# The second expert stage of a four-layer network made sparse: rows scattered to tiles of their experts, weights addressed by a register

## The chip, the cores and the metric

One core of a Trainium2 chip. The metric is the time of one execution on the device, in microseconds (us). Everything is fp32 except where bf16 is named.

## What is computed

Four layers over x (4 batches of 512 rows of 128) and a context (4 x 154 x 128). Each layer is a cross-attention (L2 adds causal self-attention) and a feed-forward part of experts, both added to x by a gate. The two expert stages that the change touches most:

```python
# L0: 8 experts, top 2, at most C = 1.25 S / E rows an expert; h = relu(x w1 + b1); out = h w2 + b2
# L1: 8 experts, top 2, no limit on an expert's rows
router_logits = x_flat @ gate_w                       # (2048, 8)
router_probs = softmax(router_logits)
top_k_probs, top_k_idx = top_k(router_probs, 2)       # then normalized to sum 1
gate_up = einsum('nd,edh->enh', x_flat, gate_up_w)    # gate_up_w (8, 128, 512)
hidden = silu(gate_up[..., :256]) * gate_up[..., 256:]
expert_out = einsum('enf,efd->end', hidden, down_w)   # down_w (8, 256, 128)
output = sum over the 2 chosen experts of expert_out * top_k_probs
# L3: 16 experts, top 2, and a shared expert
```
x_flat is the layer normalization of the residual rows. L2's and L3's experts stay dense in both kernels.

## The kernel before

The rows stand in SBUF all the time (`resid`, 16 tiles of 128 rows; a batch is QT = 4 tiles). `build` runs one block of instructions after another: setup, and for each layer an attention block (L0x, L1x, L2x with L2a, L3x) and an expert block (L0f, L1f, L2f, L3f); each ends with a barrier of all engines (L2991, L2993), so that no engine enters a block before all have left the one ahead of it. In a block each engine has its own list, written by hand, and semaphores tie them.

**L0f, sparse already.** `Dispatch` finds for each row the slots of its two experts: DVE takes the two best logits (`best`), TensorE counts the ranks with triangular matmuls (`ranks`), DVE turns them into slot numbers (`place`). `scatter` (L2091 to L2100) lets POOL write each tile of 128 rows twice with an indirect DMA into `slots_in` in DRAM, 32 in all, in three groups of tiles, `GROUPS` = (0, 8), (8, 12), (12, 16). The first group's 16 stand in the attention block L0x, whose POOL then waits until they have landed (L926). `sparse_experts` (L2121) loads the slots by SP, and its results go to `slots_out`; the next block, `wide_attention` of L1x (L232), gathers each row's two results by indirect DMAs on POOL and adds them (L593 to L749).

**L1f, dense.** `Router` (L1571) does the routing of one batch of 4 tiles at a time; the first batch's is hosted in L1x (`router.` hooks at L299, L409 and after). `experts` (L1706) goes through 32 items, a batch and an expert each: `up(item + 1)`, then `down(item)` on TensorE. An item is 2 units of 128 hidden columns; a unit is two 128x512 matmuls (L1774, L1775: weights stationary, 512 rows moving) into one of two pairs of PSUM banks, a silu on ACT (L1823) and a product on DVE (L1872). Down (L1788) is 8 matmuls, and DVE adds the expert's share with the routing weight (L1884, L1887). After a batch's last item `update_rows` (L732 to L749) adds the gated sum to the rows and takes the statistics for the next normalization (BATCH_NORM_STATS2, the centering of `resid`, BATCH_NORM_AGGREGATE).

**The end.** L3f is the same `experts` with 17 items a batch (its `rowsT` is L1646); after it `store` (L2780) writes all of `resid`, 1 MB, in a block of its own.

What `up` does in the dense stage:

```python
for k, (wg, wu, rows) in enumerate(items[item % NI][0]):
    n = units_to(item) + k
    if n >= SETS:
        pe.wait_ge(s["hid"], n - SETS + 1)
    nc.tensor.matmul(psum[0:rows, 2 * (n % 2), :], wg, xnT[b % 2][:], start=True, stop=True)
    nc.tensor.matmul(psum[0:rows, 2 * (n % 2) + 1, :], wu, xnT[b % 2][:], start=True, stop=True).then_inc(s["up"], 1)
```

## Time and profile before

| | |
|---|---|
| median of 3 runs | 1821.96 us (1820.03 to 1822.71) |
| profiled execution, its own time | 1822.82 us |
| its span, first to last instruction | 1821.1 us |
| TensorE (PE) busy | 1466.5 us, 81% of the span |
| VectorE (DVE) busy | 1058.4 us, 58% |
| ScalarE (ACT) busy | 683.6 us, 38% |
| GpSimd (POOL) busy | 394.6 us, 22% |
| mean busy share of the DMA engines | bytes moved 32.17 MB, mean 18 GB/s |
| granted TensorE clock, mean | 0.88 of full speed |

A share of busy time is a mean over all blocks, and each block has its own limit. A matmul of fp32 shows as more than one record. "Idle before" counts an engine's idle time just ahead of an instruction, and the name after it is what ended that. PEq and the like are an engine's own sequencer. SPq rows are DMAs that SP issued.

### The profile page before, as it was taken

How to read it: one execution, taken by the hardware profiler on the slowest of the kernel's cores; microseconds unless marked ns; L12 is line 12 of the kernel's file. 1: busy time of each engine (PE TensorE's matmuls, PEld its weight loads, DVE VectorE, ACT ScalarE, POOL GpSimd, SP SyncE). 2: the span in 40 equal slices, each digit the busy share in tenths (PEclk: the TensorE clock that was granted, in tenths of full speed). 3: DMA queues.
4: the chain of work that ended last, by engine and by line, in shares of the span. 5: the costliest groups of instructions: out<-in, count | busy, mean ns of one | idle time of the engine just before them, and what ended most of it. 6: DMA issues, size and time to landing. Idle time of an engine off the chain costs nothing. (4 is left out here: it accounts for less than half of the span.)

```text
span 1821.1 us, 26968 instructions
## 1 busy us (share of the span) xinstructions
PE 1466.5 (81%) x9930; PEld 886.7 (49%) x9930; DVE 1058.4 (58%) x2645; ACT 683.6 (38%) x1824; POOL 394.6 (22%) x488
## 2 busy tenths in 40 slices
PE   3677925758989979995888599888888968887997
PEld 2333414535556546664333356565554544344564
DVE  6555541154556656655454576676775964556886
ACT  3233412246656422223334355555552133332111
POOL 1000042345323300000100276767550001000000
PEclk7677867979999989996799699999998977988999
DMA  2430011140000000001000000000000010000000
GB/s 48 141 121 14 8 42 56 37 101 12 2 1 1 1 1 1 0 1 22 7 9 2 1 1 1 1 1 1 1 1 1 1 22 8 9 2 1 1 1 24
DMA packets 46823, 32.17 MB, mean 18 GB/s; under 512 B 16076, under 2 KB 41109, under 8 KB 46693
## 3 DMA queue, kind: packets, MB, share of 16 engines
q1 hardware_dynamic: 42885, 25.43, 5.6%
q0 software_dynamic: 2048, 4.20, 1.0%
q8 instruction: 80, 1.31, 0.3%
q10 hardware_dynamic: 1760, 0.82, 0.2%
q14 instruction: 50, 0.41, 0.1%
HBM read 19.80 MB, written 5.77 MB: 14 GB/s over the span
## 5 line engine op out<-in xcount | busy, mean ns | idle before, releaser
L2638 ACT ACTIVATE L2a_pr<-psum,L2a_negmax 128x512 f32<-128x512 f32 (+3 forms) x256 | 131.7, 525 | 131.2 <-DVE L2a_negmax L2708 72.6
L538 ACT ACTIVATE L1x_praw<-psum,L1x_negmax 128x154 f32<-128x154 f32 x256 | 95.9, 390 | 77.6 <-DVE L1x_negmax L629 77.5
L2506 PE MATMUL psum<-ident,L2a_pr 128*128 128x128 f32 x640 | 95.7, 299 | 34.0 <-DVE L2a_pT L2728 20.0
L2506 PEld LDWEIGHTS psum<-ident,L2a_pr 128*128 128x128 f32 x640 | 80.3, 155 | 41.0 <-issue 25.1
L311 POOL TENSOR_TENSOR L1x_pm<-L1x_praw,L1x_total 128x1024 f32<-128x1024 f32 x32 | 60.7, 1897 | 160.1 <-DVE L1x_total L635 86.9
L1462 DVE TENSOR_REDUCE L0x_negmax<-psum 128x6 f32<-128x924 f32 (+1 forms) x48 | 47.7, 1010 | 79.1 <-PE psum L1036 76.2
L1462 DVE TENSOR_REDUCE L2x_negmax<-psum 128x6 f32<-128x924 f32 (+1 forms) x48 | 47.8, 1011 | 69.8 <-PE psum L1036 54.6
L1462 DVE TENSOR_REDUCE L3x_negmax<-psum 128x6 f32<-128x924 f32 (+1 forms) x48 | 47.8, 1011 | 68.9 <-PE psum L1036 57.6
L1823 ACT ACTIVATE L1f_sg<-psum 128x512 f32<-128x512 f32 x64 | 38.2, 597 | 121.5 <-PE psum L1775 121.5
L629 DVE TENSOR_REDUCE L1x_negmax<-psum 128x4 f32<-128x616 f32 x64 | 50.8, 795 | 55.1 <-PE psum L358 51.3
L1884 DVE SCALAR_TENSOR_TENSOR L3f_acc<-psum,L3f_comb,L3f_acc 128x128 f32<-128x128 f32 x256 | 71.9, 343 | 8.3 <-PE psum L1788 5.0
L1872 DVE TENSOR_TENSOR L1f_hid<-L1f_sg,psum 128x512 f32<-128x512 f32 x64 | 43.7, 687 | 56.3 <-ACT L1f_sg L1823 56.1
L1774 PE MATMUL psum<-L1f_xnT,L1f_gu 128*128 128x512 f32 x128 | 66.7, 603 | 9.3 <-PEq L2993 9.3
L2397 POOL TENSOR_TENSOR L2a_pr<-L2a_pr,L2a_total 128x1024 f32<-128x1024 f32 x32 | 60.6, 1895 | 51.3 <-DVE L2a_total L2736 51.3
L1265 ACT ACTIVATE L2x_pT<-psum 128x512 f32<-128x512 f32 x80 | 41.3, 603 | 79.6 <-PE psum L1061 64.0
L1265 ACT ACTIVATE L0x_pT<-psum 128x512 f32<-128x512 f32 x80 | 41.2, 601 | 79.7 <-PE psum L1061 61.5
L1265 ACT ACTIVATE L3x_pT<-psum 128x512 f32<-128x512 f32 x80 | 41.2, 601 | 77.0 <-PE psum L1061 61.5
L1788 PEld LDWEIGHTS psum<-L1f_dn,L1f_hid 128*128 128x128 f32 x512 | 62.0, 192 | 14.8 <-issue 14.8
L1036 PE MATMUL psum<-L0x_k,L0x_q 32*128 32x154 f32 x384 | 44.4, 371 | 28.2 <-DVE L0x_negmax L1462 18.7
L1823 ACT ACTIVATE L3f_sg<-psum 128x512 f32<-128x512 f32 (+1 forms) x44 | 26.3, 597 | 106.6 <-PE psum L1775 106.6
L1036 PEld LDWEIGHTS psum<-L0x_k,L0x_q 32*128 32x128 f32 x384 | 34.8, 234 | 64.2 <-DVE L0x_negmax L1462 41.6
L2726 DVE COPY L2a_pT<-psum 128x768 f32<-128x768 f32 x64 | 60.8, 950 | 8.9 <-PE psum L2506 8.5
(649 smaller groups left out, 3566.3 us busy)
## 6 DMA issues: line engine op xcount, KB each, us to landing
expert_arena<-in_L_ffn_w SPq DMA_DIRECT2D x16, 256.0 KB, 5.4
L1f_gu<-in_L_ffn_gate_up_w SPq DMA_DIRECT2D x8, 256.0 KB, 3.7
slots_in<-zero SPq DMA_DIRECT2D x1, 1280.0 KB, 9.2
L0f_xs<-slots_in SPq DMA_DIRECT2D x5, 256.0 KB, 4.1
resid<-in_x SPq DMA_DIRECT2D x4, 256.0 KB, 5.7
L1f_dn<-in_L_ffn_down_w SPq DMA_DIRECT2D x8, 128.0 KB, 3.8
slots_out<-L0f_ys SPq DMA_DIRECT2D x16, 64.0 KB, 1.6
expert_arena<-in_L_ffn_w_gate_up SPq DMA_DIRECT2D x2, 512.0 KB, 5.5
```

Of the source, the lines that this page charges most:

```text
L311: nc.gpsimd.tensor_tensor(pm[:, n % 2].rearrange("p j t k -> p (j t) k"), praw[:, n % 3, :, :, 0:MAIN].rearrange("p j t k -> p (j t) k"), ...
L538: nc.scalar.activation(praw[:, n % 3, j, t, :], psum[:, 2 * u + j, x * CTX:(x + 1) * CTX], ACT.Exp, bias=negmax[:, n % 2, u, j, x:x + 1], ...
L1036: last = nc.tensor.matmul(psum[:, bank + j % 2, k * CTX:(k + 1) * CTX], q4[rows, f % QB, c, t * P:(t + 1) * P], k4[rows, c, f, 0:CTX], sta ...
L1265: nc.scalar.activation(pT[:, (n % 2) * NG + j, :], psum[:, LANES + j, :], ACT.Exp, scale=scale).then_inc(s["pt"], 1)
L1462: nc.vector.tensor_reduce(negmax[:, f % 2, half, 2 * h:2 * h + 2, off:off + count], psum[:, bank:bank + 2, 0:count * CTX].rearrange("p j ( ...
L1774: nc.tensor.matmul(psum[0:rows, 2 * (n % 2), :], wg, xnT[b % 2][:], start=True, stop=True)
L1788: last = nc.tensor.matmul(psum[:, 4 + n % 3, t * P:(t + 1) * P], hid[rows, slot, t * P:(t + 1) * P], w2, start=(m == 0), stop=(m == len(te ...
L1823: nc.scalar.activation(sg[0:rows, n % 2, :], psum[0:rows, 2 * (n % 2), :], ACT.Silu).then_inc(s["silu"], 1)
L1884: ins = nc.vector.scalar_tensor_tensor(out=to, in0=ps, scalar=comb[:, b % 2, t, col:col + 1], in1=to if k else x1[:, b * QT + t, :], op0=A ...
L2506: last = nc.tensor.transpose(psum[:, TURN + n // 4, n % 4 * P:(n % 4 + 1) * P], pr[:, m % RING, n * P:(n + 1) * P], core.ident[:])
L2638: ins = nc.scalar.activation(pr[:, i % RING, SEQ * j + lo:SEQ * j + hi], psum[:, bank + j, lo:hi], ACT.Exp, bias=negmax[:, i % RING, e:e + ...
L2726: nc.vector.tensor_copy(pT[:, q % 2, t:t + 7:3, heads, :], src[:, :, 0:3 * P].rearrange("p j (k x) -> p k j x", x=P))
```

## The change

Three things.

1. **L1f becomes sparse.** A new class `Grouped` routes in 2 groups of 1024 rows (batches 0 and 1, then 2 and 3). Each expert gets as many tiles of 128 slots as its rows need, 23 tiles always in all (1024 x 2 / 128 = 16, and at most 7 for broken ones). `place` gives the slots, `table` the list of which expert each tile has (`of`). POOL scatters 16 tile halves a group into `group_in`, SP loads them four tiles at a time ("quads", 6 a group). For each tile TensorE loads the expert's number into a register (`value_load`), does one up matmul with rows stationary and the 512 weight columns that the register addresses moving, transposes the hidden rows (2), and does 2 down matmuls with weights by register. Results go through `group_out` in DRAM; POOL gathers 8 tile halves a batch, and DVE adds them. Group 0's routing and its 16 scatters are hosted in L1x; group 1's run inside the loop of group 0's tiles. Batches 0 and 1 are summed inside group 1's loop, 2 and 3 after it.
2. **L0f.** `HOSTED` = 5 of the first group's 8 tiles are scattered in L0x, the other 3 in L0f, from rows in a buffer (`pair`) that lasts over both blocks; the wait for landing goes. Some steps of L0's routing stand in another order.
3. **The end.** The last `experts` writes each batch's rows to the output with a 256 KB DMA from SP; the statistics after them, and the `store` block, go.

Two more buffers are filled with zeros by DMA in the first attention block.

```diff
 # wide_attention (L1x)
+                    if n == 12:
+                        grouped.constants(nc.gpsimd)
+                    if n == NS - 2:
+                        grouped.scatter(nc.gpsimd, 0, rows.rearrange("p b t d -> p (b t) d"), 0, 2)
+                grouped.scatter(nc.gpsimd, 0, rows.rearrange("p b t d -> p (b t) d"), 2, 2 * QT)
...
+                    if b == B - 1:
+                        if g == 0:
+                            grouped.spread(0)
+                        if g == 1:
+                            for x in range(2):
+                                grouped.front(dve, v, x, rows[:, x])
+                        if g in (3, 4):
+                            grouped.best(dve, v, 0, g - 3, H0)
+                        if g == 5:
+                            grouped.place(dve, v, 0, H0)
+                        if g == 6:
+                            grouped.table(dve, v, 0)
 # narrow_attention (L0x)
-                    dispatch.scatter(nc.gpsimd, 0, first_rows)
-                    pool.wait_ge(dispatch.s["spread"], 16 * 2 * 2 * QT)
+                    dispatch.scatter(nc.gpsimd, 0, first_rows, 0, dispatch.HOSTED)
...
                         dispatch.best(dve, v, 0, tmp["lg"], tmp)
+                        dispatch.front(dve, v, 1, dispatch.rows)
                         dispatch.place(dve, v, 0, tmp, 0)
-                        dispatch.front(dve, v, 1, dispatch.rows)
 # experts, final = io["out"] in L3f
+                        else:
+                            if b >= 2:
+                                dve.wait_ge(stored[b - 2], 16)
+                            nc.vector.scalar_tensor_tensor(out=last_rows[b % 2][:], in0=acc[:, b % 2], scalar=core.gate[:, gate:gate + 1],
+                                                           in1=core.resid[:, b * QT:(b + 1) * QT, :], op0=ALU.mult, op1=ALU.add).then_inc(s["ready"], 1)
 # sparse_experts (L0f)
-                dispatch.scatter(nc.gpsimd, 1, dispatch.rows)
-                dispatch.scatter(nc.gpsimd, 2, xn)
+                dispatch.scatter(nc.gpsimd, 0, dispatch.pair[:].rearrange("p f t d -> p (f t) d"), dispatch.HOSTED, 2 * QT)
+                dispatch.scatter(nc.gpsimd, 1, dispatch.rows, 0, QT)
+                dispatch.scatter(nc.gpsimd, 2, xn, 0, QT)
...
                 pe.wait_ge(loaded, 16 * n_loads)
-                dispatch.ranks(pe, 1, RANK)
                 dispatch.rowsT(pe, 2, 3, xn, 3)
                 dispatch.logits(pe, 2, [xnT], LOGITS)
+                dispatch.ranks(pe, 1, RANK)
...
                 dispatch.spread(2)
+                dispatch.front(dve, v, 2, xn)
                 dispatch.best(dve, v, 1, dispatch.lg1[:], tmp[1])
-                dispatch.front(dve, v, 2, xn)
                 dispatch.place(dve, v, 1, tmp[1], RANK)
 # grouped_experts (L1f)
+                loads(0)
+                stores(0)
+                loads(1)
+                stores(1)
...
+                grouped.scatter(nc.gpsimd, 1, xn[:].rearrange("p b t d -> p (b t) d"), 0, 2 * QT)
+                for b in range(B):
+                    if b % 2 == 0:
+                        for q in range(b // 2 * QUADS, (b // 2 + 1) * QUADS):
+                            pool.wait_ge(stored[q], 16)
+                    for x in range(2 * QT):
+                        t, r = x // 2, x % 2
+                        n = b * QT + t
+                        nc.gpsimd.indirect_dma_start(out=got[:, b, x * D:(x + 1) * D], out_offset=None, in_=slots_out[b // 2],
+                                                     in_offset=bass.IndirectOffsetOnAxis(grouped.to[:, r, n:n + 1], 0)).then_inc(back[b], 16)
...
+                def up(i):
+                    q, t = quad_of(i), i % TILES % 4
+                    if t == 0:
+                        pe.wait_ge(s["st"], q + 1)
+                    if i >= len(UP):
+                        pe.wait_ge(s["hid"], i - len(UP) + 1)
+                    expert[i] = pe.value_load(grouped.of[0:1, i // TILES, i % TILES:i % TILES + 1], min_val=0, max_val=grouped.E - 1)
+                    nc.tensor.matmul(psum[:, UP[i % len(UP)], :], xsT[:, q % 2, t * P:(t + 1) * P],
+                                     w["gu"][:, bass.ds(expert[i], 1), :].rearrange("p a f -> p (a f)"), start=True, stop=True).then_inc(s["up"], 1)
...
+                    for x in range(STEPS):
+                        i = k * TILES + x
+                        if x < TILES:
+                            up(i)
+                        if x < TILES and x % 4 == 1 and x // 4 + 1 < QUADS:
+                            turn(k * QUADS + x // 4 + 1)
+                        if 0 <= x - 2 < TILES:
+                            hiddenT(i - 2)
+                        if 0 <= x - 3 < TILES:
+                            down(i - 3)
+                        if k == 0 and x == 0:
+                            grouped.logits(pe, 1, [xT[:, 0], xT[:, 1]], ROUTE)
+                        if k == 0 and x == 5:
+                            pe.wait_ge(g["lg"], 2)
+                            grouped.ranks(pe, 1, ROUTE)
```

In this order rows of TensorE's list (line of the kernel, operation, tiles, shape, count), the dense loop of L1f stands like this before, one item of an expert and a batch:

```order
L1774 MATMUL psum<-L1f_xnT,L1f_gu 128x512
L1775 MATMUL psum<-L1f_xnT,L1f_gu 128x512
L1774 MATMUL psum<-L1f_xnT,L1f_gu 128x512
L1775 MATMUL psum<-L1f_xnT,L1f_gu 128x512
L1788 MATMUL psum<-L1f_dn,L1f_hid 128x128 x8
```

In the changed kernel, one tile of 128 slots (L1f_of is the table of experts; the ISA rows are register arithmetic and addresses):

```order
L2613 TENSOR_LOAD L1f_of
L2613 ISA x2
L2614 ISA
L2614 MATMUL psum<-L1f_gu,L1f_xsT 128x512
L2622 MATMUL psum<-ident,L1f_hid 128x128 x2
L2631 ISA
L2631 MATMUL psum<-L1f_dn,L1f_hidT 128x128
L2631 ISA
L2631 MATMUL psum<-L1f_dn,L1f_hidT 128x128
```

32 items of 12 matmuls have become 46 tiles of 5, each with a register load ahead of its first, and one more matmul a tile that turns the loaded rows.

POOL's list from L0x into L0f, before (the ISA row between is the block change):

```order
L2099 DMA slots_in<-L0x_xn,L0f_to 6656x128 x16
L849 UNCONDITIONAL_BRANCH
L2993 ISA
L2169 UNCONDITIONAL_BRANCH
L2099 DMA slots_in<-L0f_rows,L0f_to 6656x128 x8
L2099 DMA slots_in<-L0f_xn,L0f_to 6656x128 x8
```

And in the changed kernel:

```order
L2140 DMA slots_in<-L0f_pair,L0f_to 6656x128 x10
L867 UNCONDITIONAL_BRANCH
L3474 ISA
L2210 UNCONDITIONAL_BRANCH
L2140 DMA slots_in<-L0f_pair,L0f_to 6656x128 x6
L2140 DMA slots_in<-L0f_rows,L0f_to 6656x128 x8
L2140 DMA slots_in<-L0f_xn,L0f_to 6656x128 x8
```

Six of the first group's DMAs have moved behind the block change.

SP's list in L1f of the changed kernel (before, SP has nothing there):

```order
L2568 DMA L1f_xs<-group_in 128x4x128 x5
L2568 DMA L1f_xs<-group_in 128x3x128
L2575 DMA group_out<-L1f_ys 128x4x128 x5
L2575 DMA group_out<-L1f_ys 128x3x128
L2568 DMA L1f_xs<-group_in 128x4x128 x5
L2568 DMA L1f_xs<-group_in 128x3x128
L2575 DMA group_out<-L1f_ys 128x4x128 x5
L2575 DMA group_out<-L1f_ys 128x3x128
```

The second group's loads stand behind all stores of the first.

## Rows read from the trace of the kernel before

**Rows 1.** Windows: us, busy time (and count) by engine, PEclk, DMA share, GB/s
```profile
652.00:829.00 177.00, 172.79 (x804) 110.44 (x804) 102.67 (x309) 43.28 (x74) 0.00 (x0) 0.99 0.00 1
290.00:297.00 7.00, 6.22 (x16) 3.93 (x15) 0.69 (x1) 2.11 (x4) 0.00 (x0) 0.52 0.41 108
104.00:112.00 8.00, 5.10 (x28) 2.75 (x28) 4.62 (x15) 0.24 (x1) 0.00 (x0) 0.50 0.00 0
```
The five busy times are of PE, PEld, DVE, ACT and POOL.

**Rows 2.** Timeline of the second expert stage's ends: start, duration, engine, line
```profile
651.98 0.17 DVE L220 TENSOR_SCALAR std<-stat 128x16 f32<-128x16 f32 x1 [1.20 <-PEq L2993]
652.13 2.04 PE L1774 MATMUL psum<-L1f_xnT,L1f_gu 128*128 128x512 f32 x2 [9.31 <-PEq L2993]
655.41 1.02 PE L1774 MATMUL psum<-L1f_xnT,L1f_gu 128*128 128x512 f32 x2
...
819.47 1.02 PE L1774 MATMUL psum<-L1f_xnT,L1f_gu 128*128 128x512 f32 x2
...
821.18 3.73 PE L1788 MATMUL psum<-L1f_dn,L1f_hid 128*128 128x128 f32 x32
...
828.56 0.17 DVE L749 TENSOR_SCALAR stat<-L1f_mv 128x8 f32<-128x8 f32 x1
```

**Rows 3.** Timeline of the first expert stage, SP and PE: slots loaded and turned
```profile
286.76 2.91 SPq L2161 DMA_DIRECT2D L0f_xs<-slots_in  x5
289.84 1.09 PE L2182 MATMUL psum<-ident,L0f_xs 128*128 128x128 f32 x4 [19.89 <-DMA L0f_xs<-slots_in]
```

**Rows 4.** Timeline of POOL: the first, the 17th and the last scatter
```profile
233.68 1.22 POOL L2099 DMA_INDIRECT slots_in<-L0x_xn,L0f_to  x1 [216.97 <-DVE L0f_to L2088]
...
265.56 0.96 POOL L2099 DMA_INDIRECT slots_in<-L0f_rows,L0f_to  x1 [11.72 <-DVE L0f_to L2088]
...
284.50 0.95 POOL L2099 DMA_INDIRECT slots_in<-L0f_xn,L0f_to  x1 [0.30 <-issue]
```

**Rows 5.** Groups by shape elsewhere in the kernel: busy, mean ns | idle before
```profile
L2638 ACT ACTIVATE L2a_pr<-psum,L2a_negmax 128x256 f32<-128x256 f32 x64 | 29.4, 472 | 31.5 <-DVE L2a_negmax L2702 31.5
L2268 DVE TENSOR_TENSOR L0f_ys<-psum,L0f_b2b 128x256 f32<-128x256 f32 x8 | 3.4, 425 | 37.3 <-PE psum L2200 37.3
L2254 DVE COPY L0f_xsT<-psum 128x512 f32<-128x512 f32 x5 | 3.5, 691 | 22.3 <-PE psum L2182 22.3
```

**Rows 6.** Timelines of routing for the first stage, and a table load in L1x
```profile
222.57 0.23 DVE L2008 TENSOR_TENSOR L0x_ra<-psum,L0f_gate_b 128x64 f32<-128x64 f32 x1
...
226.58 0.17 DVE L2051 TENSOR_TENSOR L0f_gap<-L0x_ra 128x8 f32<-128x8 f32 x1
230.02 0.23 DVE L2075 TENSOR_SCALAR L0x_ra<-psum 128x64 f32<-128x64 f32 x1 [3.27 <-PE psum L2063]
...
232.59 0.17 DVE L2088 CAST L0f_to<-L0x_ra 128x16 uint32<-128x16 f32 x1
...
220.58 1.06 PE L1999 MATMUL psum<-L0f_gate,L0x_rb 128*128 128x8 f32 x8
...
640.55 1.28 ACT L549 ACT_TABLE_LOAD   x1
```

**Rows 7.** Timeline of DVE: the sum of one batch's gathered results in L1x
```profile
366.71 1.22 DVE L593 TENSOR_TENSOR L1x_praw<-L1x_praw,slot_wt 128x1024 f32<-128x1024 f32 x1
...
371.13 0.17 DVE L749 TENSOR_SCALAR stat<-L1x_mv 128x8 f32<-128x8 f32 x1
```

**Rows 8.** Timeline of the end, then DMA issues: KB each, us from issue to landing
```profile
1812.01 0.75 DVE L732 SCALAR_TENSOR_TENSOR L3f_new<-L3f_acc,gate,resid 128x512 f32<-128x512 f32 x1
...
1815.62 0.40 SPq L2786 DMA_DIRECT2D out_x<-resid  x1
...
slots_out<-L0f_ys SPq DMA_DIRECT2D x16, 64.0 KB, 1.6
...
out_x<-resid SPq DMA_DIRECT2D x1, 1024.0 KB, 5.1
```

**Rows 9.** Waits, from 1500 us on: in total, times, longest
```profile
PE psum L1646 <- DVE L3f_xn L1635: 2.1, 2, 1.1
```

More of the change, by code:

```diff
@@ L477, in _ @@
                             query(n + NG, H0)
-                        elif g in (2, 4):
+                        elif g in (2, 3, 5):
                             pe.wait_ge(s["pt"], 2 * (n - 2) + 1)
                             if g == 2:
-                                router.rowsT(pe, 0, xn[:, 1], H0)
-                            else:
-                                router.logits(pe, 0, router.xnT, H0)
+                                grouped.rowsT(pe, 0, rows[:, 0], H0)
+                            if g == 3:
+                                grouped.logits(pe, 0, turned_rows, H0)
+                            if g == 5:
+                                grouped.ranks(pe, 0, H0)
                     if n >= 3 and n % 2 and n - 2 < NS:
@@ L492, in _ @@
                             value(b, 2 + g, H1)
+                        if b == B - 1 and g == 2:
+                            grouped.rowsT(pe, 1, rows[:, 1], H1)
                         if b + 1 < B:
@@ L1722, in experts @@
     s = {n: nc.alloc_semaphore(f"{L}_{n}") for n in (
-        "var", "sd", "vec", "up", "silu", "hid", "down", "acc", "const")}
+        "var", "sd", "vec", "up", "silu", "hid", "down", "acc", "const", "ready")}
+    stored = [nc.alloc_semaphore(f"{L}_stored{b}") for b in range(B)]
     r, oh, eq, score, gap = router.s, router.oh, router.eq, router.score, router.gap
@@ L1743, in experts @@
         new = sb("new", [P, QT, D])
+        last_rows = [new, sb("new1", [P, QT, D])] if final is not None else []
         parts = sb("parts", [P, QT, 6])
@@ L1751, in experts, with _ @@
         with nc.Block() as block:
+            @block.sync
+            def _(sp):
+                if final is not None:
+                    for b in range(B):
+                        sp.wait_ge(s["ready"], b + 1)
+                        sp.dma_start(final[b].rearrange("(t p) d -> p t d", p=P), last_rows[b % 2][:]).then_inc(stored[b], 16)
+                    for b in range(B):
+                        sp.wait_ge(stored[b], 16)
             @block.gpsimd
@@ L2089, in place, with scatter @@
         nc.vector.tensor_scalar(self.core.slot_of[:, :, t0:t1], number, float(self.slots - 1), None, ALU.min).then_inc(s["of"], 1)
-    def scatter(self, pool, k, rows):
-        t0, t1 = self.GROUPS[k]
+    def scatter(self, pool, k, rows, t0, t1):
+        first = self.GROUPS[k][0]
         pool.wait_ge(self.zeroed, 16)
@@ L2096, in scatter @@
         pool.wait_ge(self.s["slot"], k + 1)
-        for n in range(t0, t1):
+        for n in range(first + t0, first + t1):
             for r in range(2):
                 pool.indirect_dma_start(out=self.slots_in, out_offset=bass.IndirectOffsetOnAxis(self.to[:, r, n:n + 1], 0),
-                                        in_=rows[:, n - t0, :], in_offset=None).then_inc(self.s["spread"], 16)
+                                        in_=rows[:, n - first, :], in_offset=None).then_inc(self.s["spread"], 16)
 def work_tiles(flat, n, E):
@@ L2777, in _ @@
                         keep_rows(core, v, b, new, parts, mv, dest=x1)
-def store(core, io):
-    stored = core.sem("stored")
-    with core.nc.Block() as block:
-        @block.sync
-        def _(sp):
-            sp.dma_start(io["out"].rearrange("b (t p) d -> p (b t) d", p=P), core.resid[:]).then_inc(stored, 16)
-            sp.wait_ge(stored, 16)
 def row(ap):
@@ L2996, in build @@
                     moe[1](router)
-        store(core, io)
 def kernel(**inputs):
```

416 lines of the change are left out of this document (384 added, 32 removed).

## The prediction

> **What bounds the kernel now.** I read the page's busy times first (TensorE 81% of the span), then the windows by stage, then the timeline at each stage's ends, since the blocks run one after another and the change touches only some. In the second expert stage TensorE works 172.8 of 177.0 us at granted clock 0.99 [rows 1]: it is bound by its matmuls and nothing else, and it multiplies all 2048 rows by all 8 experts where 2 are chosen. It lasts from its first instruction at 651.98 to the end of its last at 828.73, 176.7 us [rows 2]. The first expert stage has another bound: TensorE stands idle 19.9 us until rows come in [rows 3], which waits for POOL's 32 indirect DMAs [rows 4].
>
> **The second stage, counted anew.** Full clock: two 128x512 weight-times-rows matmuls take 821.18 - 819.47 = 1.71, one 0.86; 32 records of down matmuls take 3.73, so a 128x128 matmul (2 records) 0.23 [rows 2]. Four 128x128 transposes took 1.09 in a stretch at clock 0.52 [rows 1, 3]; at full clock I take half, 0.14 each. A tile of 128 slots now needs one up matmul (0.86), two hidden transposes (0.27), two down (0.47) and its share of turning the rows (0.14): 1.74. ACT has 0.47 silu, 0.47 copy and a quarter of a 0.6 copy, DVE 0.43 for the product and a quarter of 0.69 [rows 5], both under 1.2, so TensorE sets the pace if the register loads hide. 46 tiles x 1.74 = 80.0. Around them:
> - start: SP issue to first matmul 3.1 [rows 3], then 12 transposes at half clock, 3.3, and hand-offs: 6.7;
> - the clock coming up again at the head of each group: this stage's third 128x512 matmul started at 655.41, 3.28 after its first at 652.13, where 1.71 is normal [rows 2]; 2 x 1.6 = 3.2;
> - routing of group 1 inside group 0's loop. DVE: best 4.2 in two pieces, place 2.7, both from the first stage's routing [rows 6], each less the 0.7 of transposes and down matmuls that TensorE still has: 2 x 1.4 + 2.0. TensorE: logits (1.06 for half of them [rows 6]) and ranks, 3.3. Together 8;
> - the sums of batches 0 and 1 inside group 1's loop. The same steps took 366.71 to 371.30 = 4.6 [rows 7]; 2 x (4.6 - 0.7) = 7.8;
> - draining each group (silu, product, transposes, copy, down, hand-offs): 2 x 2.3 = 4.6;
> - turnover: SP sends group 1's loads behind all of group 0's stores, so last results 0.69, issue 0.9, landing 3.1, four transposes and a copy: 6.0;
> - tail: results 0.69, issue 0.43, store landing 2.5 (between 1.6 for 64 KB and 5.1 for 1 MB [rows 8]), 16 gathers by POOL at the period of its scatters, (284.50 - 265.56)/15 = 1.263 [rows 4], 20.2, last landing 1.6, sum 4.6: 30.0.
> Sum 146.3, against 176.7: **-30.4**. Two thirds of what TensorE saves is given back, most of it in the tail, where every engine but POOL is idle.
>
> **What the layer before it takes over.** Group 0's routing moves into the last batch of the L1x attention. DVE gets best 4.2, place 2.7, a table of some 1.0 and four more row normalizations, 1.1; the router's own best, on half the tiles, goes, some 2.8: +6.2. ACT gets two table loads of 1.28 [rows 6]. TensorE gets 2.7. DVE's gaps there may hide it all, and at worst some 11 come out; I take **+6**, its DVE share. POOL's 16 scatters (20.2) start after ranks at about 625 and end by 646, before the block's end at 650.8, which costs nothing; if routing is late by 5 they set the end.
>
> **First expert stage.** POOL's idle time between the 16th and 17th scatter is 11.72 [rows 4]. It comes from the wait for landing, the block change and the second group's routing. Now 10 scatters stand ahead of the block change and 6 after, so the gap is the change itself, 1.2 as between the stages [rows 2]: -10.5. The start comes 1.3 earlier, since the 1.1 us normalization moves out of the way. But in the new block the second group's slots come some 8.8 after its start (normalizing first, logits before ranks), and six scatters last 7.6: +1.3. Sum **-10.2** with 0.3 for hand-offs; 32 scatters at 1.263 are the floor.
>
> **Last stage and end.** The batches' waits for normalized rows, 2.1 [rows 9], go with the statistics that stood ahead: **-2.1**. At the end, 1812.01 + 0.75 is followed now by a 256 KB write (2.9, between the same two sizes) instead of statistics, a block change and 5.1 for 1 MB issued at 1815.62 [rows 8]: 1815.8 against 1820.7, **-4.9** (-3.5 to -6.2). Filling two more buffers with zeros writes 3 MB; at 5.1 per MB [rows 8] this is 15 us of the ring, most of it beside an attention stage that loads nothing then: **+0.5** (0 to 9).
>
> Sum: -30.4 + 6 - 10.2 - 2.1 - 4.9 + 0.5 = -41.1, from the profiled execution's 1822.8 to 1781.7; the median is 0.9 lower, so **1781**.
>
> **The unknown price: the register.** No row of before has a load of a register from SBUF, or a matmul whose weights are addressed by one. Below: nothing, if the sequencer runs ahead while TensorE works off its queue. Above: a round trip as long as a 64 KB DMA, 1.6 [rows 8], with the queue drained, per tile. The nearest row is the 1.20 us of a block change [rows 2], which is sequencer work alone. I take zero: the conditions the load waits for (the product two tiles back) are met 1.3 us before the queue is empty, 1.74 less the 0.4 by which the product lags, so 1.2 fits.
> The Trainium skill, "DMA: Bandwidth & Descriptors", Latency and other measured facts, gives a floor of about 600 ns for a tensor_load; with nothing hidden the stage would be an estimated 46 x 0.6 = 27.6 us longer by it and the kernel at 1808. That is rival 1's case; no row here bears on the figure.
>
> **The rivals.**
> 1. *Register loads partly exposed.* The loads start only when the tile's wait is over; 0.71 of queued work covers 1.20: 0.49 x 46 = +23, **1804** (with 1.6 instead of 1.2: +41, 1822, no gain). For it: every tile's up matmul stands behind its own load, none is fetched ahead of the loop. Against: the margin above.
> 2. *Slower: the load drains TensorE.* If it waits for all matmuls before it, and the address is used at once, each tile pays it all: 46 x 1.2 = 55, **1836**; at 1.6, 1855. It decides from 41.1/46 = 0.89 us per tile. For it: an in-order queue, and five address instructions more per tile. Against: the block change already holds a barrier that a load does not.
> 3. *Slower: the clock.* TensorE's granted clock was 0.50 (1.2 GHz) in a stretch in which it was busy 64%, and 0.99 (2.4 GHz) in the stage at 98% [rows 1]. Should gaps between short matmuls keep it at the lower level, 80 us of tiles become 159: **1860**. The tile loop as counted leaves TensorE few gaps, which speaks against.
> The Trainium skill, "TensorE: Matmul & The Clock Gate", HAM oscillation, says that waits inside a loop can bring the clock down again; that would make rival 3's result more likely, and the rows above agree only for a stage with much idle time.
> 4. *POOL slower.* Gathers of scattered rows at 2.3 instead of 1.26 would add 17 in the tail: **1798**.
> 5. *The change does less at the head.* Hidden sums and routing cost nothing beside TensorE and the L1x routing hides: -18, **1763**.
>
> **How the numbers follow.** As forecast (1763 to 1800) 0.60; rival 1 0.19; rival 2 0.07; rival 3 0.03; rival 4 0.06; rival 5 or below 0.05. The range goes from 1763 to 1813: it leaves out rivals 2 and 3, a third of rival 1 and half of 5, under 0.2. Within 0.2% of 1822 (3.6 us, about what a measurement tells from no change) lies only the worst of rival 1: 0.01. Slower: rivals 2 and 3, less rival 2's shares near break-even: 0.09. Faster: 0.90.
>
> **What would show it.** In the windows of the changed kernel: TensorE at clock near 1.0 in the tile loops and a tile every 1.74 us (over 2.2 is rival 1, over 2.6 rival 2; half clock rival 3); in the chain of waits TensorE idle until register or sequencer work; the stage near 146 us, with POOL's 16 gathers alone at its end for 20 us; no gap over 3 us among the 32 scatters of the first stage; the attention before within 6 us of its old length. The prediction is wrong if the sparse stage is longer than 165 us or shorter than 130.

## The result and the profile after

The changed kernel takes 1810.46 us (median of 6, 1806.63 to 1811.44) against 1819.78 for the one before (6 runs beside them): ratio 0.9933, interval 0.9913 to 0.9954. Faster, as forecast, and inside the range of 1763 to 1813, but by 9 to 12 us where 41 were forecast. The profiled execution is 1811.44, its span 1809.7.

The blocks run one after another, so the first instruction of each tells where the time went. From these starts (rows that end in PEq in the timeline) of one profiled execution each, in us; the last two columns, the changed kernel once more in set 3 and a version of it in set 4, are explained with the experiments:

| block | before | after | after, in set 3 | g2_order |
|---|---|---|---|---|
| L0x and L0f | 332.5 | 323.6 | 321.1 | 327.2 |
| L1x | 306.4 | 313.8 | 306.6 | 314.6 |
| L1f, the second expert stage | 177.8 | 169.2 | 141.2 | 131.1 |
| L2x | 181.7 | 189.4 | 186.2 | 182.0 |
| L2a | 375.8 | 373.6 | 373.6 | 375.9 |
| L2f | 88.9 | 88.1 | 88.1 | 88.5 |
| L3x | 180.6 | 182.3 | 182.5 | 180.9 |
| L3f to the end | 164.3 | 156.8 | 156.9 | 157.6 |

Two blocks are off: L1f gained 8.6 instead of 30.4, and L2x, whose code is the same, lost 7.7. Together these are 29.5 of the 29.7 us by which the profiled execution missed the forecast.

The windows of the sparse stage, after (busy time of PE, PEld, DVE, ACT, POOL; PEclk; DMA share; GB/s; answers to [rows 1]):

```profile
650.00:662.00 12.00, 7.96 (x31) 6.62 (x31) 2.94 (x11) 3.67 (x6) 0.00 (x0) 0.50 0.45 127
662.00:683.00 21.00, 20.24 (x121) 12.86 (x121) 10.70 (x39) 7.66 (x21) 4.74 (x5) 0.89 0.08 26
683.00:705.00 22.00, 12.81 (x38) 7.50 (x37) 3.26 (x9) 4.01 (x11) 10.65 (x12) 0.61 0.15 48
705.00:722.00 17.00, 14.82 (x83) 10.05 (x81) 5.52 (x12) 6.47 (x19) 0.00 (x0) 1.00 0.19 56
...
735.00:750.00 15.00, 5.85 (x25) 3.95 (x24) 0.94 (x3) 2.28 (x7) 6.35 (x7) 0.73 0.13 36
750.00:765.00 15.00, 15.00 (x77) 9.90 (x77) 6.53 (x13) 6.76 (x19) 0.00 (x0) 0.93 0.12 37
...
792.00:819.00 27.00, 0.00 (x0) 0.00 (x0) 8.89 (x26) 0.00 (x0) 15.39 (x16) 0.52 0.14 39
```

In two stretches TensorE does 38 and 25 matmul records where the stretches behind them hold 83 and 77 in 17 and 15 us. Both have POOL at its indirect DMAs (12 and 7 in them). In the two stretches behind them POOL has nothing to do, and TensorE is busy 14.8 of 17 and 15 of 15 us. Between 765 and 792, left out above, it is busy 18.3 of 27 us, also without POOL: there it waits for the sums of batches 0 and 1. The last 27 us are the tail of gathers.

The timeline of the sparse stage, after, all engines in order of time (answers to [rows 2]). The clean loop, then inside the first bad stretch:

```profile
711.06 1.02 PE L2614 MATMUL psum<-L1f_gu,L1f_xsT 128*128 x2
711.92 0.38 PE L2622 MATMUL psum<-ident,L1f_hid 128*128 128x128 f32 x2
712.14 0.61 PE L2631 MATMUL psum<-L1f_dn,L1f_hidT 128*128 x4
712.58 1.02 PE L2614 MATMUL psum<-L1f_gu,L1f_xsT 128*128 x2
```

```profile
682.58 1.03 PE L2614 MATMUL psum<-L1f_gu,L1f_xsT 128*128 x2
...
688.90 0.64 PE L2622 MATMUL psum<-ident,L1f_hid 128*128 128x128 f32 x2
...
691.28 0.38 ACT L2675 ACTIVATE L1f_sg<-psum 128x256 f32<-128x256 f32 x1 [5.27 <-remote]
691.76 0.42 DVE L2710 TENSOR_TENSOR L1f_hid<-L1f_sg,psum 128x256 f32<-128x256 f32 x1 [1.75 <-issue]
...
694.09 0.38 ACT L2681 ACTIVATE L1f_hidT<-psum 128x256 f32<-128x256 f32 x1 [2.42 <-remote]
694.61 1.22 PE L2631 MATMUL psum<-L1f_dn,L1f_hidT 128*128 x4 [5.08 <-issue]
```

A clean tile takes 712.58 - 711.06 = 1.52 us. In the bad stretch the silu at 691.28 belongs to the up matmul of 682.58, which was over at 683.6: ACT waited for it until 7.7 us later. "Remote" is a release for which the profile shows no instruction at that time. DVE follows ACT at once (691.66 to 691.76) and TensorE follows ACT at once (694.47 to 694.61). In these rows only what TensorE gives to others is late.

The other stages. First POOL's scatters of L0f (answers to [rows 4]), then the end (answers to [rows 8]), then the head and tail of the sparse stage:

```profile
228.98 1.22 POOL L2140 DMA_INDIRECT slots_in<-L0f_pair,L0f_to  x1 [212.41 <-DVE L0f_to L2129]
...
245.11 0.96 POOL L2140 DMA_INDIRECT slots_in<-L0f_pair,L0f_to  x1 [3.52 <-POOLq L3474]
...
256.54 0.96 POOL L2140 DMA_INDIRECT slots_in<-L0f_rows,L0f_to  x1 [4.14 <-DVE L0f_to L2129]
...
650.35 0.17 DVE L2371 TENSOR_SCALAR std<-stat 128x8 f32<-128x8 f32 x1 [1.19 <-PEq L3474]
...
656.77 2.07 PE L2614 MATMUL psum<-L1f_gu,L1f_xsT 128*128 x2
...
788.65 0.56 DVE L2718 COPY L1f_ys<-psum 128x384 f32<-128x384 f32 x1 [1.46 <-PE psum L2631]
...
792.04 0.95 POOL L2592 DMA_INDIRECT L1f_got<-group_out,L1f_to  x1 [48.86 <-DMA group_out<-L1f_ys]
...
1805.38 0.75 DVE L1948 SCALAR_TENSOR_TENSOR L3f_new<-L3f_acc,gate,resid 128x512 f32<-128x512 f32 x1
1806.15 0.37 SPq L1782 DMA_DIRECT2D out_x<-L3f_new  x1
```

The gap of 11.72 among the scatters [rows 4] has become 3.52 and 4.14. The sparse stage's first up matmul comes 6.4 after its start (6.7 forecast), and from the last results at 788.65 to the next block at 819.52 it is 30.9 (30.0 plus the block change forecast). So the stage's start and its tail came as forecast, and the trouble lies in the tile loops.

**The sign was in the trace of before.** At the head of L1x, POOL issues 24 gathers in a row while TensorE projects keys and values. The timeline there, before:

```profile
357.79 1.88 PE L345 MATMUL psum<-projections,ctxt 128*128 128x512 f32 x4
...
363.31 0.69 DVE L621 TENSOR_TENSOR L1x_vt<-psum,quad 128x512 f32<-128x512 f32 x1 [2.11 <-remote]
...
366.10 0.69 DVE L621 TENSOR_TENSOR L1x_vt<-psum,quad 128x512 f32<-128x512 f32 x1 [2.10 <-remote]
```

TensorE was done at 359.7, and the DVE instructions that wait for it start at 363.3 and 366.1. POOL's first gather had started at 346.3.

### The profile page after: what moved, and what is told of

Its sections match the earlier page's. It is cut to its first block and busy times, and to the rows that moved or that the text cites. A ratio compares the mean times of both kernels' runs of the same rounds, so it can differ in the third digit from the quotient of the medians.

```text
span 1809.7 us, 26729 instructions
## 1 busy us (share of the span) xinstructions
PE 1394.7 (77%) x9650; PEld 836.8 (46%) x9650; DVE 1010.7 (56%) x2467; ACT 687.9 (38%) x1864; POOL 458.1 (25%) x577
## 5 line engine op out<-in xcount | busy, mean ns | idle before, releaser
L2993 PE MATMUL psum<-ident,L2a_pr 128*128 128x128 f32 x640 | 89.7, 286 | 34.1 <-DVE L2a_pT L3215 20.0
L2993 PEld LDWEIGHTS psum<-ident,L2a_pr 128*128 128x128 f32 x640 | 74.9, 147 | 41.2 <-issue 23.5
L2140 POOL DMA_INDIRECT slots_in<-L0f_pair,L0f_to x16 | 15.6, 977 | 220.2 <-DVE L0f_to L2129 212.4
L2614 PE MATMUL psum<-L1f_gu,L1f_xsT 128*128 x92 | 60.2, 745 | 7.9 <-DVE L1f_hid L2710 5.3
L2710 DVE TENSOR_TENSOR L1f_hid<-L1f_sg,psum 128x256 f32<-128x256 f32 x46 | 19.3, 421 | 81.1 <-ACT L1f_sg L2675 51.5
L1821 PEld LDWEIGHTS psum<-expert_arena,L3f_hid 64*128 64x128 f32 x512 | 48.6, 187 | 24.6 <-issue 20.5
```

The lines of the kernel that those rows point to most:

```text
L1821: last = nc.tensor.matmul(psum[:, 4 + n % 3, t * P:(t + 1) * P], hid[rows, slot, t * P:(t + 1) * P], w2, start=(m == 0), stop=(m == len(te ...
L2614: nc.tensor.matmul(psum[:, UP[i % len(UP)], :], xsT[:, q % 2, t * P:(t + 1) * P], w["gu"][:, bass.ds(expert[i], 1), :].rearrange("p a f -> ...
L2993: last = nc.tensor.transpose(psum[:, TURN + n // 4, n % 4 * P:(n % 4 + 1) * P], pr[:, m % RING, n * P:(n + 1) * P], core.ident[:])
```

## The experiments

**Theory T (trains):** while POOL issues many indirect DMAs one behind the other, TensorE's completions, and the signals they carry, come late. **Rival R (registers):** the register loads get slow beside POOL's DMAs. A further rival: each indirect DMA costs a fixed time wherever it stands.

### Set 1

**e1_const**, registers out:

```diff
-                    expert[i] = pe.value_load(grouped.of[0:1, i // TILES, i % TILES:i % TILES + 1], min_val=0, max_val=grouped.E - 1)
+                    expert[i] = i % grouped.E
...
```

(The weights of both matmuls are then addressed by this constant.)

> The expert of each tile is a constant (tile number modulo 8) in place of the register load; TensorE's other work, POOL's trains of indirect DMAs and all waits stay. It leaves out the addressing by the routing, so rows go through experts that are not theirs. Theory T (trains): while POOL issues many indirect DMAs one behind the other, signals that TensorE gives reach ACT and DVE some 2 us late each or worse, register loads or not: the two stretches with long waits of ACT on TensorE stay (each about 10 us), the sparse stage stays within 4 us of 169, the kernel at 1805 to 1813. Rival R (registers): the loads of registers are what gets slow beside POOL's trains: both stretches go, the stage is at most 150 us and the kernel at 1787 to 1795.

Measured: 1808.74 us, one run. ACT's long waits stay, and so do both bad stretches; the waits of e1_const (total, times, longest):

```profile
ACT L1f_sg L2675 <- remote: 19.8, 4, 6.6
DVE L1x_y L665 <- remote: 13.2, 1, 13.2
```

R as the cause of the stretches falls. But the stage is 155.4 us where T had said 165 to 173, so T missed too, and among late signals of changing length this run can't say what the registers cost.

**e3_late**, the sums moved:

```diff
-                        if k == 1 and x in (13, 19):
-                            added((13, 19).index(x))
-                for b in (2, 3):
+                for b in range(B):
                     added(b)
```

> The sums of batches 0 and 1 stand behind the tile loop, ahead of those of 2 and 3, where DVE waits for POOL's last 16 gathers. My working has them at 2 x 3.9 us of TensorE's time in the loop, and nothing behind it, since 9.2 us of DVE fit in the 20 us of gathers: the stage 7 to 10 us shorter, the kernel at 1801 to 1804. If the sums cost nothing in the loop: no change, 1810.

Measured: 1801.78, ratio 0.989 (0.9839 to 0.9941), stage 156.5. Against the changed kernel's 0.9933 that is 8 us, as expected, but the intervals overlap, so it isn't shown; and the stage is 12.7 shorter than the changed kernel's, more than the 7 to 10 expected. As in e1_const, late signals of changing length are in it.

**e2_pace**, on top of e3_late:

```diff
                     for x in range(2 * QT):
                         t, r = x // 2, x % 2
                         n = b * QT + t
+                        if b < 2 and r == 0:
+                            pool.wait_ge(s["up"], TILES + 1 + 3 * (b * QT + t) - (b * QT + t) // 4)
```

> As e3_late, and the 16 gathers of batches 0 and 1 go in pairs, each pair held until TensorE has begun some three more tiles. Theory T: no train is longer than two there, so the waits of 5 to 9 us of ACT on TensorE at the middle of group 1 go: 8 to 12 us faster than e3_late, about 1792 to 1795. Rival R, or any theory in which the number of DMAs and not their density counts: the same time as e3_late within 2 us. The scatter train of group 1 (16 in a row) is left as it is, and its stretch of waits should stay in both.

Measured: 1792.49, ratio 0.9832 (0.9786 to 0.9878), stage 144.5: 9 us by the medians and 12 in the stage, in the range of T, with the same 16 gathers. The intervals of the ratios overlap here too. The windows of e2_pace:

```profile
684.00:712.00 28.00, 18.92 (x80) 11.95 (x79) 5.43 (x14) 7.31 (x22) 12.74 (x14) 0.82 0.17 52
...
727.00:779.00 52.00, 41.94 (x206) 26.98 (x204) 20.87 (x48) 18.77 (x52) 19.20 (x20) 0.90 0.26 71
```

The train of scatters, left as it was, still costs TensorE 9 of 28 us.

**e4_train**, the kernel before with a train where it had none:

```diff
+                if L == "L1f":
+                    pool.wait_ge(s["up"], 16)
+                    for x in range(24):
+                        nc.gpsimd.indirect_dma_start(out=train[:, x, :], out_offset=None, in_=core.train_from,
+                                                     in_offset=bass.IndirectOffsetOnAxis(core.slot_of[:, x % 2, x // 2:x // 2 + 1], 0)).then_inc(s["train"], 16)
+                    pool.wait_ge(s["train"], 16 * 24)
...
```

(Left out: the lines that make the buffer and the semaphore.)

> The kernel before, with 24 extra gathers by POOL in one train in the dense second stage, into a buffer that nothing reads (from the stage's 16th unit on). No register is loaded there by TensorE. Theory T: in about the second half of those 30 us, and until the last gather has gone, ACT's silu and DVE's accumulation wait for TensorE for 2 us and more at a time though its matmuls are over; the stage gets 8 to 20 us longer, the kernel 1828 to 1840. Rival R: nothing of this, the stage stays at 177 us within 1, the kernel at 1820 to 1823.

Measured: 1848.36, one run, 27 above before's median in this set; its L1f block lasts 199.1 instead of 177.8. That is 21 us, a little more than the 8 to 20 of T. The timeline of e4_train's TensorE:

```profile
711.67 1.40 PE L1795 MATMUL psum<-L1f_dn,L1f_hid 128*128 128x128 f32 x10
715.53 0.27 PE L1795 MATMUL psum<-L1f_dn,L1f_hid 128*128 128x128 f32 x1 [2.46 <-issue]
716.22 0.27 PE L1795 MATMUL psum<-L1f_dn,L1f_hid 128*128 128x128 f32 x1 [0.42 <-issue]
718.32 0.37 PE L1795 MATMUL psum<-L1f_dn,L1f_hid 128*128 128x128 f32 x1 [1.83 <-issue]
719.01 0.37 PE L1795 MATMUL psum<-L1f_dn,L1f_hid 128*128 128x128 f32 x1 [0.33 <-issue]
721.12 0.37 PE L1795 MATMUL psum<-L1f_dn,L1f_hid 128*128 128x128 f32 x1 [1.73 <-issue]
```

These 16 records are 8 matmuls in one group with no wait among them. A record takes 0.12 in the clean loop [rows 2]; here two of them, one matmul, come every 2.8 us. So it is TensorE's own progress that is held, not the receiver. The train ran from 694.2 to 724.3. The first late completion is one that DVE gets at 702.8, up to 706 TensorE is still busy all the time, and DVE's next result from TensorE after 709 comes at 728.2.

### Set 2

**e5_merged** keeps the change's small parts, and has L1f and L1x of before:

```diff
-        layers.append((lambda early, a=a: Grouped(core, early, a[0], a[1], a[2], a[3], a[4], a[6]),
-                       lambda grouped, a=a: grouped_experts(grouped, a[0], a[1], 5, a[2], a[3], a[5])))
+        layers.append((lambda early, a=a: Router(core, early, a[0], a[1], 8, a[2], a[3]),
+                       lambda router, a=a: experts(router, a[0], a[1], 5, a[4], a[2], a[3])))
...
```

(Left out: L1x hosts the old routing again, and the two buffers of `Grouped` with their zeros are gone.)

> The small changes alone: the second expert stage and the attention ahead of it are those of before, the first stage's scatter in two blocks, the output by batches and no store block are those of the change. Their share of the change is by the two traces -8.9 us up to the end of the first expert stage and -7.5 in the last, so 16 us faster than before, ratio 0.991. If so, the sparse stage by itself brought no more than the block's own 8.6 us, and L1x and L2x took 15 back. The L2x block (181.7 before, 189.4 after, with the same code) is 182 here if the sparse stage's surroundings lengthen it, 186 or more if the earlier start or chance does.

Measured: 1803.29, ratio 0.9932 (0.9909 to 0.9954), 14 us, and L2x at 182. The expected 16 us are missed by little. Its ratio is that of the whole change in the first measurement, which would mean that the sparse stage brought nothing there; but the two ratios are of different sets, and what follows shows that sets can differ.

**e8_dense_fours**, e4_train's 24 gathers in trains of four:

```diff
                     for x in range(24):
+                        if x and x % 4 == 0:
+                            pool.wait_ge(s["up"], (19, 21, 24, 26, 29)[x // 4 - 1])
```

> As the dense kernel with 24 extra gathers (1848 us), but they go in trains of four with breaks of some 2 to 3 us, held by TensorE's progress. Theory T, density: the stage is back at 177 to 180 and the kernel at 1819 to 1825. Rival: each indirect DMA costs TensorE a fixed time wherever it stands: 1848 again, within 4.

Measured: 1817.51, one run, beside 1816.89 of before: nothing.

**e6_order**, on top of e2_pace (the scatter has a `held` semaphore, for group 1 `s["up"]`):

```diff
+            if held and t and t % 2 == 0:
+                pool.wait_ge(held, 9 + 2 * t)
...
                 loads(0)
-                stores(0)
-                loads(1)
-                stores(1)
+                stores(0, 4)
+                loads(1)
+                stores(4, 2 * QUADS)
```

> As e2_pace (1792.5), and group 1's 16 scatters go in trains of four, held by TensorE's tiles, and SP issues group 1's loads ahead of the last two stores of group 0. Theory T: the 28 us around the train, in which TensorE was busy 19, shrink by 7 to 9; and the 8 us between the groups' tiles shrink by 3 to 5: 1779 to 1783. If the signals are late in trains of four too: no more than the order's 3 to 5, 1788 to 1790.

Measured: 1761.39, ratio 0.9694 (0.9655 to 0.9734), stage 130.3: far more than either theory.

**e7_break**, on top of e6_order:

```diff
-                grouped.scatter(nc.gpsimd, 0, rows.rearrange("p b t d -> p (b t) d"), 2, 2 * QT)
+                grouped.scatter(nc.gpsimd, 0, rows.rearrange("p b t d -> p (b t) d"), 2, 5)
+                pool.wait_ge(s["yr"], B)
+                grouped.scatter(nc.gpsimd, 0, rows.rearrange("p b t d -> p (b t) d"), 5, 2 * QT)
```

> As e6_order, and the 12 scatters at the end of L1x are cut in 6 and 6, the second six held until DVE has taken TensorE's last result of the block. Theory T: DVE's wait there, ended 4 us after TensorE's last matmul, ends at once: 3 to 4 us faster than e6_order, 1776 to 1780. If that wait has another cause: the same as e6_order, or 1 to 2 slower, since the scatter ends later.

Measured: 1764.76, ratio 0.9714 (0.9698 to 0.973): no gain, where T had expected 3 to 4 us. DVE had nothing to gain in this set: in e6_order too, with its 12 scatters in a row, it starts as soon as TensorE is done.

All of set 2 had something in common that no edit explains. The head of L1x, the same 24 gathers in every kernel, took 33.6 to 34.0 us from the block's first instruction to the first row maximum; in before, after and all of set 1 it had taken 39.7 to 40.8. So set 2 could not be laid beside set 1.

### Set 3: the same kernels side by side

f1_train is e4_train, f2_fours is e8_dense_fours, f3_after is the changed kernel and f4_order is e6_order, unaltered.

> The dense kernel with the train of 24 gathers once more, now beside the kernel with the same 24 in fours, since the two stood in different calls and the head of the L1x block (24 gathers in a row in every kernel) told these apart: its first DVE maximum came 40 to 41 us after the block's start in all kernels of the first call and of before and after, 34 in all of the second. If the train costs by itself: again 20 us or more over the dense kernel. If the second call's chip simply does not have the effect: no more than 3 over it where the L1x head is at 34.

> The dense kernel with 24 gathers in fours. Theory T: within 3 us of the dense kernel on any chip, also where f1_train is 20 slower. Rival (a chip without the effect explains all): as slow as f1_train.

> The changed kernel unaltered, for its stages on this chip. Theory T with a cost that depends on the chip: where the L1x head takes 34 us, the changed kernel is faster than 0.9933 of before, down to 0.980; where it takes 40, 0.993.

> The version with gathers in pairs, scatters in fours and loads ahead of stores, beside the changed kernel. Its sparse stage 128 to 132 us as before; if the pacing does the work, the changed kernel's stage beside it is 155 or more.

Measured, with the L1x head at 34 to 35 us: f1_train 1815.57 and f2_fours 1817.05, one run each (before 1816.61), their L1f blocks 179.3 and 177.9; f3_after 1770.22, ratio 0.9743 (0.9727 to 0.976), its stage 141.2; f4_order 1762.75, ratio 0.9696 (0.9672 to 0.972), stage 133.0. The expected "155 or more" beside it is missed, and so is f3_after's "down to 0.980": trains cost nothing here. The same part of the train, from 12 to 33 us after its first gather, in the two executions of the same dense kernel, e4_train and then f1_train:

```profile
706.00:727.00 21.00, 7.58 (x26) 4.12 (x24) 1.89 (x8) 0.60 (x1) 14.08 (x15) 0.77 0.32 50
```

```profile
695.70:716.70 21.00, 21.00 (x100) 13.35 (x99) 12.66 (x41) 5.18 (x9) 13.61 (x15) 1.00 0.30 49
```

With 15 gathers in both stretches TensorE is busy 7.6 us in the one and all 21 in the other. The changed kernel shows the same: from 6 to 28 us after its train of scatters begins it was busy 12.8 of 22 us (683 to 705, above), and in f3_after:

```profile
674.00:696.00 22.00, 21.43 (x118) 14.50 (x116) 7.67 (x19) 9.69 (x28) 10.54 (x11) 1.00 0.28 85
```

So a train *can* hold TensorE up, and there are conditions in which it does not. All kernels of one set ran on one chip, and each set was of one kind throughout. Sets 2 and 3, without late completions, ran on the same chip; sets 1, 4 and 5, with them, on three others. The kernel before pays for late completions too: its head of L1x, with 24 gathers, took 40.8 us, and 34.0 in e8_dense_fours, which has the same code there.

### Sets 4 and 5

g1_after is the changed kernel, g4_train is e4_train, g2_order is e6_order. **g3_const** is e6_order with e1_const's edit.

> The changed kernel a third time. Its ratio to before was 0.9933 where the long trains came with late signals (sparse stage 169 us) and 0.9743 where they didn't (141). It should come out as one of these two, within 0.003, and the four kernels of this call should all be of the same kind.

> The dense kernel with its extra train, as the sign of the kind: about 20 to 30 us slower than the dense kernel where g1_after is at 0.993, nothing where it is at 0.974.

> Gathers in pairs, scatters in fours, loads ahead of two stores. Theory T: this version has no long train beside TensorE in the sparse stage, so the stage is 133 us or less in either kind; where g1_after is at 0.993, this one is at 0.975 to 0.980 (its L1x block keeps its trains of 24 and 12), and where g1_after is at 0.974, at 0.970.

> As g2_order with a constant expert for each tile, so rows go through experts that are not theirs. If the 46 register loads are hidden: the same as g2_order, within 3 us. If each costs 0.1 to 0.5 us: 5 to 23 us faster.

Measured: this set was of the kind with late completions (before 1826.61; g4_train 1843.64, one run, 17 above it where 20 to 30 were expected, with the L1f block at 199.2 as in e4_train). g1_after 1811.35, ratio 0.9923 (0.9905 to 0.9941), stage 169.1: it repeats the first measurement. g2_order 1776.93, ratio 0.9742 (0.9707 to 0.9777), stage 131.1. The windows of g1_after and then of g2_order, the same part of the stage:

```profile
690.00:712.00 22.00, 13.01 (x40) 7.59 (x39) 3.65 (x9) 4.04 (x12) 10.34 (x11) 0.61 0.15 48
```

```profile
680.00:705.00 25.00, 24.08 (x130) 15.88 (x129) 9.61 (x24) 11.00 (x33) 12.83 (x15) 1.00 0.22 69
```

With 15 scatters in trains of four TensorE is busy 24.1 of 25 us; with 11 in one train, 13.0 of 22. The whole difference of 0.018 between g1_after and g2_order holds three edits (late sums, pacing, order of loads). In set 3, where trains cost nothing, the same three were worth 0.0047. The rest, some 0.013 or 24 us (give or take 9 by the intervals), is what pacing saves where completions are late. This settles T in its narrower form, and it speaks against a fixed cost of each indirect DMA: both kernels have the same 16 scatters and 16 gathers beside the loops. The dense kernel with its gathers in fours ran only in sets 2 and 3, so it says nothing of this.

g3_const 1770.97, ratio 0.9699 (0.9661 to 0.9736), stage 124.0 against 131.1: 7.1 us for 46 tiles, 0.15 each. This rests on one profiled execution of each kernel: by the medians it is 6 us, with intervals that overlap, and the stage of g2_order's kernel took 130.3 to 133.0 in three executions. The matmul groups of g2_order and then g3_const show most of it as TensorE's idle time ahead of the up and down matmuls (the last columns; 2.7 of the 5.5 us come back ahead of the matmuls that turn the rows, 17.9 and then 20.6):

```profile
L2619 PE MATMUL psum<-L1f_gu,L1f_xsT 128*128 x92 | 50.8, 637 | 4.3 <-issue 4.2
L2636 PE MATMUL psum<-L1f_dn,L1f_hidT 128*128 x184 | 29.3, 284 | 2.0 <-ACT L1f_hidT L2686 1.8
```

```profile
L2619 PE MATMUL psum<-L1f_gu,L1f_xsT 128*128 128x512 f32 x92 | 49.7, 626 | 0.7 <-ACT L1f_xsT L2674 0.7
L2636 PE MATMUL psum<-L1f_dn,L1f_hidT 128*128 128x128 f32 x184 | 28.5, 278 | 0.1
```

Set 5: h2_break is e7_break. **h1_head** is that and:

```diff
-                for b in range(3):
+                for b in range(2):
                     fetch(b, 0, 2 * QT)
...
+                    if n < 4:
+                        fetch(2, 2 * n, 2 * (n + 1))
...
-                    if n == 2:
+                    if n == 5:
                         summed(2)
```

> e7_break once more. In a call of the kind with late signals (sign: the first DVE maximum of L1x 40 us after the block's start) theory T wants its L1x block 4 us shorter than g2_order's 314.6, since DVE need not wait behind the train of 12, and a ratio of 0.970 to 0.973; in the other kind 0.970 to 0.972 as measured.

> As h2_break, and of the 24 gathers in a row at the head of L1x the last 8 go in pairs into the first four units. Theory T: where signals come late, the head (41 us to the first maximum) shrinks by 3 to 6 us and the ratio is 0.002 to 0.003 lower than h2_break's; where they don't, nothing changes, within 1.5 us.

Measured, again with late completions: h2_break 1771.89, ratio 0.9727 (0.9697 to 0.9756); h1_head 1775.99, ratio 0.9739 (0.9706 to 0.9772). The wait of DVE at the end of L1x, in the waits of g2_order and then the timeline of h2_break:

```profile
DVE L1x_y L665 <- remote: 13.2, 1, 13.2
```

```profile
635.05 1.15 PE L415 MATMUL psum<-L1x_bos,ones 1*128 1x128 f32 x8
...
636.24 0.69 DVE L667 TENSOR_TENSOR L1x_y<-psum,L1x_xn 128x512 f32<-128x512 f32 x1 [8.16 <-PE psum L415]
...
643.91 0.96 POOL L2517 DMA_INDIRECT group_in<-L1x_got,L1f_to  x1 [0.30 <-issue]
...
649.81 0.17 DVE L2373 TENSOR_SCALAR std<-stat 128x8 f32<-128x8 f32 x1 [5.49 <-PEq L3479]
```

With the break DVE starts at once, as before; in the changed kernel it started 4.2 after TensorE's end. The same instruction in f3_after, with the 12 scatters in a row as in g2_order, but in a set without late completions:

```profile
631.94 0.69 DVE L665 TENSOR_TENSOR L1x_y<-psum,L1x_xn 128x512 f32<-128x512 f32 x1 [8.16 <-PE psum L413]
```

But in h2_break the block ends 13.6 later instead of 9.1, so of 6 us the block keeps 1.4 (313.3 against 314.6), where T wanted 4. The last rows show why: DVE waits 5.49 for the block change, where 1.19 is normal, and POOL issued its last scatter 5.9 before the new block began. It is 5.9 in e7_break and h1_head too, so in either kind: a block change close behind POOL's indirect DMAs takes longer, and the break moved them there. The head of L1x shrank by 1.2 only, where T expected 3 to 6, and h1_head's ratio isn't lower than h2_break's. Neither version is faster than g2_order beyond the intervals.

## Why the prediction was wrong

- **The step that failed** is where POOL's work was costed at nothing: 16 scatters in L1x "which costs nothing", and the tile loops counted for TensorE alone beside POOL's 16 scatters and 16 gathers. What the runs showed in its place: where completions come late, TensorE is held up beside these trains, and the stage takes 169.2 instead of 146.3. The trains inside the loops are worth some 24 us of the kernel by g2_order against g1_after, and by the same kernel in set 3 the stage is 28 shorter. The 12 scatters at the end of L1x are worth 5. Why a chip has late completions at all stays open. No rival had it either: rival 4 thought of POOL itself as slow, and its DMAs kept their 1.25 us (16 gathers in 20 us). Where trains cost nothing (set 3), the same sum is near: 41 us forecast, 46 measured, and the stage 141.2 against 146.3. That the first measurement fell into the forecast range at all is luck: what was missing there is not one of the things that the range was made for.
- **The register**, taken at zero between 0 and 1.6 us: 0.15 a tile. Rival 1 (0.49) and rival 2 (1.2) fall. The Trainium skill, "DMA: Bandwidth & Descriptors", Latency and other measured facts, has a floor of some 600 ns; no run shows how long the load itself takes, and with that floor an estimated three quarters of it were hidden, where the margin of 1.3 us had said all.
- **A tile** was 1.52 in the clean loop (up 0.86, transposes 0.22, down 0.44, from the starts above), plus 0.11 as its share of turning, against 1.74 forecast: transposes and turning were cheaper than half of their time at the lower clock. This made up for most of the registers.
- **Rival 3, the clock:** 1.00 in the clean window from 705 to 722 (2.4 GHz). In the two bad stretches it fell to 0.61 and 0.73, as a consequence: in e4_train it was still 1.00 from 694 to 706, when the first completion was already late.
- **Start 6.4 (6.7), tail 30.9 with the block change (31.2):** right. The sums in the loop (7.8) are 8 by the ratio of e3_late, which isn't clear of noise.
- **L1x** +7.4 (+6 forecast): right in sum, in part by luck. From the last row maximum to the next block it took 36.4 us instead of 30.3; in f3_after it took 31.4, so 5.0 of it is DVE's late completion, which had not been thought of. In set 3 the block grew as much, by 7 to 8 (306.6 against 298.8 and 299.5), 6.3 of it between the first and the last row maximum of the last batch, where the routing is.
- **L0f** -8.9 for L0x and L0f together (-9.7 with the fills), with gaps of 3.52 and 4.14 where 1.2 and 1.3 stood in the sum; an earlier first scatter (228.98 instead of 233.68, 1.3 forecast) made up for them. That was luck: the first gap is 3.5 in e3_late, f3_after, g1_after and h2_break too, in either kind, while in g1_after, the same kernel, the first scatter stands at 233.20, and the two blocks take 327.1.
- **End** -7.5 in L3f (-7.0): right. 256 KB landed in 2.4 (2.9).
- **L2x** +7.7, forecast 0. TensorE's granted clock fell for a part of the block; the windows 120 to 135 us after its start, before and then after:

```profile
949.75:964.75 15.00, 12.12 (x100) 5.98 (x96) 8.93 (x9) 4.36 (x9) 0.00 (x0) 0.89 0.00 0
```

```profile
939.50:954.50 15.00, 12.59 (x76) 6.66 (x72) 7.30 (x7) 3.49 (x7) 0.00 (x0) 0.63 0.00 0
```

One dense kernel had 181.4, 186.0 and 181.3 in e4_train, f1_train and g4_train, so it comes and goes between executions of the same code, and where L2x was long, L2a was in most executions 2.3 shorter. The changed kernel had it in all three of its profiled executions. What sets it off was not tried.

## What to carry to other kernels

Work of POOL that issues indirect DMAs back to back is not free for TensorE: look in the trace for waits on TensorE that end microseconds after its matmul, and for releasers that the profile calls remote, before you put such trains beside a busy loop. Cut them into trains of four or fewer, held by the loop's own progress. Don't move them close to the end of a block: POOL's last one held the block change up in every version that did so. Where an effect may depend on the chip, put the untouched kernel into every set, and find a stretch that all kernels share to tell the kinds apart; set 2 alone would have told a wrong story.

The version g2_order beats both kernels in either kind: 0.974 of before against 0.992 where completions are late, 0.970 against 0.974 where they aren't.

## What was not expected of the hardware

- Twenty-four indirect gathers in a row slowed TensorE from 0.23 us a matmul (two records of 0.12) to one every 2.8 us, from some 12 us after the train's start until 4 us after its end, in sets 1 and 4 (21 us on the block in both, 27 and 17 on the whole kernel), and not at all in set 3. Sixteen scatters did the same beginning 6 us into the train. Trains of four with breaks of 1.8 us and more did nothing (g2_order).
- A block change took 5.49 us instead of 1.19 where POOL had issued its last indirect DMA 5.9 us before the new block began, in sets 2 and 5 alike.
- The Trainium skill, "SBUF — State Buffer", Who interferes with whom, says "DMA never contends with a compute engine." TensorE's progress above speaks against that, as a statement on time, for DMAs issued by POOL, and the measurement decides; that the two contend for SBUF is not shown. By which path it happens is open: whether the loading of TensorE's instructions or the carrying of signals is held up was not tried. So is whether the recording of the execution takes part, since every timed execution was recorded, and whether the kind belongs to the chip, as the two sets on one chip suggest, or to something set when a program is loaded.
- A register loaded from SBUF for each tile, with addresses made from it, cost 0.15 us a tile of 1.5 us of TensorE's work (g2_order against g3_const).
